# VectorE copies attention sums and routed weights ahead of the fourth batch's norm; GpSimd makes its additions before its query copies

## The reference, cut to what matters

```python
h = _layernorm(x, axis=-1) * (1 + ca) + sa
x = x + ga * attention(h)        # 16 heads of 8, causal, partial rotary, T = 512
h = _layernorm(x, axis=-1) * (1 + cb) + sb
x = x + gb * ffn(h)
# ffn: h @ Wm + bm is cut into 8 slices of 16 per row ("tokens"); logits = t @ expert_emb
#      softmax over 16 experts, the best two kept with their weights,
#      each expert gelu(t @ W1 + b1) @ W2 + b2, weighted sum, then @ Wo + bo
```

## Time and profile before

| | us |
|---|---|
| median of 3 runs (lowest, highest) | 398.37 (398.05, 399.06) |
| profiled execution | 399.35 |
| its span | 397.5 |
| TensorE busy | 339.4 (85%) |
| VectorE busy | 287.7 (72%) |
| ScalarE busy | 256.8 (65%) |
| GpSimd busy | 134.2 (34%) |

### The profile page before, as it was taken

The page is one execution under the profiler, slowest core; times in us unless marked ns, Lnnn a source line. Parts: engine busy times, 40 slices in busy tenths (PEclk is TensorE's granted clock), DMA queues, the critical chain, the costliest instruction groups (busy, mean ns, idle before and its releaser), DMA issues.

```text
span 397.5 us, 7269 instructions
## 1 busy us (share of the span) xinstructions
PE 339.4 (85%) x2637; PEld 158.0 (40%) x2668; DVE 287.7 (72%) x590; ACT 256.8 (65%) x297; POOL 134.2 (34%) x175
## 2 busy tenths in 40 slices
PE   3659687888798599988998899988899898879996
PEld 3425244545464344433644444433554323132123
DVE  5879868997889957787489677876569546973334
ACT  7570443535178658874558878864567997968981
POOL 6246207201302604672110624742204025532500
PEclk9957789999999979999999999999999999999999
DMA  7334123200026045540116155530123255815550
GB/s 272 94 68 77 41 43 54 42 1 3 4 49 98 17 123 133 143 102 7 31 37 101 54 137 133 148 62 3 30 39 42 82 137 144 125 47 138 151 135 26
DMA packets 27115, 31.53 MB, mean 79 GB/s; under 512 B 6780, under 2 KB 17788, under 8 KB 27068
## 3 DMA queue, kind: packets, MB, share of 16 engines
q1 hardware_dynamic: 23372, 28.57, 31.2%
q0 software_dynamic: 3456, 2.39, 2.9%
q10 hardware_dynamic: 252, 0.11, 0.2%
HBM read 3.57 MB, written 1.05 MB: 12 GB/s over the span
## 4 chain that ended last, share of the span: by engine, by line
PE 55%; DVE 21%; issue 8%; ACT 6%; DMA 4%; POOL 3%; SPq 2%; DVEq 0%; ACTq 0%; POOLq 0%
PE misc L1294 18%; PE acc L1294 18%; PE big L1294 17%; DVE mx L1032 8%; ACT ring L770 5%; PE misc L1316 2%; DMA block<-qk_turned 1%; DMA tstack<-tp 1%; SPq L517 1%; DMA cc<-in_pack_c 1%; SPq L492 1%; POOL block L446 1%; POOL gm L670 1%; DVE xn L976 1%; DVE gm L1152 1%
## 5 line engine op out<-in xcount | busy, mean ns | idle before, releaser
L770 ACT ACTIVATE ring<-big 128x1024 f32<-128x1024 f32 (+2 forms) x225 | 198.5, 928 | 94.5 <-PE big L1294 93.3
L1032 DVE TENSOR_REDUCE mx<-misc 128x1 f32<-128x512 f32 (+7 forms) x155 | 87.9, 588 | 25.1 <-PE misc L1294 23.1
L1294 PE MATMUL acc<-ring,cb 128*32 128x512 f32 x512 | 68.3, 609 | 1.5 <-DVE gm L1152 1.5
L1294 PE MATMUL big<-dense,block 128*128 128x448 bf16 (+7 forms) x249 | 54.2, 317 | 5.8 <-ACT ring L770 5.6
L1294 PE MATMUL big<-tstack,w1s 128*128 128x512 bf16 x178 | 53.0, 387 | 4.8 <-ACT ring L770 3.1
L1294 PE MATMUL misc<-dense,block 128*128 128x320 bf16 (+7 forms) x167 | 42.6, 318 | 8.7 <-DVE mx L1032 8.3
L1152 DVE SCALAR_TENSOR_TENSOR gm<-acc,cb,gm 128x512 f32<-128x512 f32 (+1 forms) x41 | 30.0, 733 | 24.5 <-PE acc L1294 19.4
L446 POOL DMA_DIRECT2D block<-qk_turned x66 | 39.4, 601 | 21.6 <-DMA tstack<-tp 20.7
L1294 PEld LDWEIGHTS big<-dense,block 128*128 128x128 bf16 x256 | 30.8, 149 | 30.7 <-ACT ring L770 16.0
L1294 PE MATMUL acc<-ring,vals 128*32 128x64 f32 (+7 forms) x512 | 40.1, 414 | 0.4
L1294 PEld LDWEIGHTS misc<-dense,block 128*128 128x128 bf16 x170 | 21.0, 150 | 48.3 <-DVE mx L1032 39.2
(11 more groups left out here) (163 smaller groups left out, 459.9 us busy)
## 6 DMA issues: line engine op xcount, KB each, us to landing
gm<-wT SPq DMA_DIRECT2D x64, 256.0 KB
dense<-qk SPq DMA_DIRECT2D x42, 64.0 KB
tstack<-tp SPq DMA_DIRECT2D x18, 128.0 KB, 4.4
block<-qk_turned POOLq DMA_DIRECT2D x66, 32.0 KB, 3.2
xs<-in_x SPq DMA_DIRECT2D x4, 256.0 KB, 8.0
ca<-in_pack_a SPq DMA_DIRECT2D x1, 769.0 KB, 7.7
out<-lg SPq DMA_DIRECT2D x3, 256.0 KB, 2.3
dense<-tp SPq DMA_DIRECT2D x6, 128.0 KB, 8.9
```

The costliest lines, as they stand in the source:

```text
L770: act.activation(dst, src, func, scale=scale).then_inc(s["ring_read"], 1)
L1032: dve.tensor_reduce(mx[:, g, k:k + n, blk], src, AX.X, ALU.max).then_inc(s["misc_read"], 1)
L1294: return pe.matmul(dst, lhsT, rhs, start=start, stop=stop)
```

## The change

Two orders are changed, and one wait is added. VectorE's change bears on turn 0 alone, since its turn 1 has no norm of batch 3 and keeps its order. GpSimd's bears on turns 0 and 1.

```diff
@@ gpsimd, loop over b @@
                 fold_experts(here)
                 rsqrt(2 * b + 3, 1)
-                stack_q(b + 2)
+                wait_read(pool, here, "lg")
                 fold_out(b + 1, here)
                 add_bias(here)
+                stack_q(b + 2)
                 if b + 3 < NB:
                     rsqrt(2 * b + 4, 0)
                 stack_k(b + 2, b)
@@ vector, loop over b @@
                 route(here)
+                divide(here, b + 1, 0)
+                take_sum(b + 1)
+                take_weights(here)
                 if b + 3 < NB:
                     statistics(xs[:, b + 3], b + 3, 2 * b + 4, 0, norm_link)
-                divide(here, b + 1, 0)
+                divide(here, b + 1, 1)
                 if b + 3 < NB:
                     normalise(xs[:, b + 3], 2 * b + 4, 0, norm_link)
-                take_sum(b + 1)
-                take_weights(here)
-                divide(here, b + 1, 1)
                 values(here, b + 2, b)
                 experts_out(here, experts_at(b), ahead=True)
```

## The result

| | us |
|---|---|
| before, 8 runs | 398.31 median (397.26 to 400.15) |
| after, 8 runs | 394.12 median (393.86 to 396.80) |
| ratio of after to before | 0.9911, 95% interval 0.9894 to 0.9928 |
| after, profiled execution | 393.95, span 392.1 |

The forecast was 393.2 in 392.3 to 395.6, and faster. The medians differ by 4.2 us; the ratio says 3.5, between 2.9 and 4.2. The two profiled executions differ by 5.4 in their spans. Two of the nine executions of e3, its profiled one among them, took 479 and 1677 us and are left out.

What follows compares the result with a forecast made beforehand. TensorE was taken to bound the kernel, idling 2.89 us at turn 0's seam behind VectorE's chain; lateness 3.04 plus clock 2.19 gave -5.23, GpSimd's part 0: 393.2 us, range 392.3 to 395.6.

Steps and rivals of the forecast that it cites:

- Turn 1 as the model of turn 0: Turn 0's seam, router end to first expert output, becomes like turn 1's, which lacks the norm: 5.23 us gained.
- Lateness, 3.04: TensorE's transposes of the sums in turn 0 start 3.04 us late against turn 1; VectorE's new order regains that.
- Clock, 2.19: After standing still at turn 0's seam, TensorE runs at its lower clock; without the long idle, 2.19 us is gained.
- What is late next: VectorE's batch-3 norm, now between weights and values in turn 0, makes values 0.2 us late; counted 0, up to 0.2.
- Rival 1: The norm becomes the wait: statistics still last 3.34 us, values 1.7 late, gain 3.5, time 394.9; chance 0.09.
- Rivals 2 and 3: Clock stays low at the seam, 395.3 us, 0.06; or another equal wait behind line 1071, no change, 398.4, 0.06.
- GpSimd's additions: cost 0, router 0.56 to 0.61 longer: Turns 0 and 1: additions during token copies slow VectorE's router by 0.56 and 0.61 us, fully covered, price 0.
- rival 4: Additions hold VectorE's router up to 4.93 us in either turn, TensorE stalls and loses clock: +6.5, 404.9 us; chance 0.05.
- The sum against the median: The profiled execution's gain, 399.35 to 394.1, carried to the median: 398.37 to 393.1, forecast 393.2.

Runs made afterwards that it cites:

- e3: Changed kernel, batch-3 statistics again right behind the router, only the normalise step left behind sums and weights: 394.62 us, ratio to before 0.9919.
- e1: Changed kernel with GpSimd's old order restored, so VectorE's change alone: 394.26 us, ratio to before 0.9904.
- e5: Changed kernel plus five unused VectorE reductions ahead of the copy of the sums in turn 1, stall 0.82 us: 394.72 us, one execution.
- e6: Changed kernel plus seven unused VectorE reductions ahead of the copy of the sums in turn 1, stall 2.00 us: 398.12 us, one execution.
- e2: Changed kernel with VectorE's old order restored, so GpSimd's change alone: 397.07 us, ratio to before 0.9967.
- e10: Kernel before, with TensorE's transposes of the first sums done six times in turn 0, 2.2 us more work: 397.12 us, ratio 0.9974.
- e4: Kernel before, run again unchanged for a second trace, 12 runs: 398.26 us, ratio 1.0001.
- e11: Changed kernel, with TensorE's transposes of the first sums done six times in turn 0: 398.02 us, ratio to before 0.9981.
- e7: Changed kernel, with GpSimd's sums of halves one product earlier everywhere, late stage included: 397.09 us, ratio to before 0.9971.

## Why the prediction was right, step by step

- *Turn 1 as the model of turn 0.* Right: both seams last 7.61 us after, at 1.00, and e1 has the whole gain by VectorE's order alone.
- *Lateness, 3.04.* Right in size. Measured from the start of the transposes of `second` to those of `yT`, the three traces of the kernel before need 5.70, 5.28 and 5.59 us, the changed one 2.66: 3.04, 2.62 and 2.93.
- *Clock, 2.19.* The mechanism was right: e5 and e6 leave it out and make it by the length of the stall alone. The size was read from one execution: by the prediction's own reckoning it is 2.19, 1.11 and 2.14 us in three. The split is a little off as well: by e2, e5 and e10 some 0.5 us of what is called lateness belongs to the clock, which leaves the sum of both as it was.
- *What is late next.* Right. The norm fits; the values are 0.11 us late, where up to 0.2 was allowed, and no gap of TensorE follows them. Rival 1 did not come: the statistics took 1.87 us, not 3.34. Rivals 2 and 3 did not come either, by the clock of 1.00 and the first output's end at 139.31.
- *GpSimd's additions: cost 0, router 0.56 to 0.61 longer.* Right: 12.05 and 12.04, and neither TensorE nor the seam shows it. The lock of the Trainium skill's "SBUF — State Buffer", section "Who interferes with whom", is in the trace in kind, one instruction of the router going from 0.69 to 1.67 us, and GpSimd takes the larger part: its four additions last 4.94 us, 1.2 more than in the old place, while the router loses 0.53. So rival 4 did not come. By e2 this half, alone, is worth 1 us, by e1 nothing beside the other.
- *The sum against the median.* This was the step that was off. The profiled execution of before was 1.1 us above the middle of its kind (span 397.5; the 12 of e4 lie from 394.6 to 398.4 with their middle near 396.5), and that of after was at the low end of its own. I carried the gain of one execution over to the median. The traces say where the difference lies (behind this list).
- *Lateness that the seam of before hid.* The sum leaves this out: VectorE's chain waits for nothing that TensorE does between the logits and the end of attention, so where the clock falls there, the seam of before takes up a part (1.6 us in e2's trace), and the changed kernel pays it whole. A fall ahead of the logits delays both chains and is not hidden. e10 and e11 show this with work in place of the clock. So the gain differs from one execution to the next, and only its middle can be compared with the medians.

**Where the two spans differ.** Line 651, GpSimd's first instruction of a turn, before and after:

```profile
105.31 0.41 POOL L651 TENSOR_TENSOR bofg<-cb,gate 128x128 f32<-128x128 f32 x1
```

```profile
104.28 0.41 POOL L651 TENSOR_TENSOR bofg<-cb,gate 128x128 f32<-128x128 f32 x1
...
189.63 0.41 POOL L651 TENSOR_TENSOR bofg<-cb,gate 128x128 f32<-128x128 f32 x1 [6.15 <-DVE lg L1159]
```

Of the 5.4 us between the spans, 1.03 lie in the opening, ahead of anything that was changed, and 4.51 in turn 0; turn 1 gives -0.14. In turn 0 the stretch from the transposes of `second` to the end of the first output is 5.22 us shorter, as forecast, and the stretch ahead of it 0.71 longer, for the changed kernel's clock is 0.79 between 100 and 108 (1.00 in the kernel before). That the profiled execution came out at 393.95 against a forecast of 394.1 is therefore in part luck. Over the three traces of the kernel before, the seam's loss against the changed kernel's is 5.22, 3.72 and 5.06 us, 4.7 in the mean. Ahead of the seam these three take 27.56 to 27.58 us from line 651; of the seven traces with VectorE's new order and no added work, two take that, four 0.7 to 0.9 more, and e1 3.5 more. So an estimate from these traces is 4.7 less 0.8 for the usual fall, 3.9 us, inside the 3.5 to 4.2 that the ratio and the medians give. It takes the kernel before to have no such fall, as in its three traces.

Open: how often the clock falls ahead of the seam. In the three traces of the kernel before and in e10's it is 1.00 between 96 and 104 us, in seven of the nine others used here it is lower; between 124 and 128 it falls in e1, e2 and e11. These are too few to say whether that is chance. No part of the change lies ahead of the first of these times; if the falls do come with the changed program, they are a part of its price that no run here explains.

## What to carry to other kernels

If the same stage runs twice, once with and once without a piece of work, lay one over the other: the offset gives the gain, and the rows of the second what is late next. A stall gained back on an engine is worth what it is in the average execution: take several traces, since a stall swallows lateness that comes before it, and removing it uncovers that. Move an instruction past a shared queue in one stage only, after looking at what stands behind it in the others (e7).

## What the runs showed of the hardware

- After pauses of 2.00 to 2.89 us at this place TensorE's clock fell to the lower of its levels for a while (e6 and three traces of the kernel before), and against the same stretch at full clock behind a short pause that cost about 1.5 to 2.7 us; after pauses of 0.28, 0.48 and 0.82 us it did not fall (e2, e10, e5).
- The cost differs between executions of one kernel: 1.6 us behind 2.45 us of pause, 2.6 behind 2.76 and 2.89.
- More work for TensorE made the kernel before no slower, and by the ratio (0.9974, 0.9950 to 0.9999) about 1 us faster, at 2.2 us of added transposes; in the trace the clock then stayed at 1.00 over the seam.
- A VectorE TENSOR_TENSOR of 32x128 took 2.31 us instead of 0.28 beside GpSimd's additions, and began 0.9 us before these did, while GpSimd was issuing copies. Without the additions behind them, the same copies did not stretch it.
